# Two eight-expert stages on sorted rows, with the routing inside the attentions ahead of them

## The reference

```python
def _L1_ffn_ref(x, gate_w, w1, w3, w2):          # F = 512
    probs = jax.nn.softmax(jnp.einsum('btd,de->bte', x, gate_w), axis=-1)
    expert_weights, expert_indices = jax.lax.top_k(probs, 2)
    expert_weights = expert_weights / expert_weights.sum(-1, keepdims=True)
    for i in range(8):
        wi = jnp.where(expert_indices == i, expert_weights, 0.0).sum(-1)
        h = jax.nn.silu(x @ w1[i]) * (x @ w3[i])
        out = out + (h @ w2[i]) * wi[..., None]
...
def _L2_ffn_ref(x, Wg, W1, W2, W3):              # H = 256
    top_v, top_i = jax.lax.top_k(jnp.einsum('bsd,ed->bse', x, Wg), 2)
    probs = jax.nn.softmax(top_v, axis=-1)
    for e in range(8):
        w_e = jnp.sum(probs * (top_i == e), axis=-1)
        h1, h2 = x @ W1[e].T, x @ W2[e].T
        out = out + ((h1 * jax.nn.sigmoid(h1) * h2) @ W3[e].T) * w_e[..., None]
```

## Time and profile before

| | us |
|---|---|
| median of 3 runs (lowest, highest) | 1563.43 (1560.48, 1563.63) |
| profiled execution | 1563.46 |
| its span, first to last instruction | 1561.6 |

### The profile page before, as it was taken

The page is one execution under the profiler, slowest core; times in us unless marked ns, Lnnn a source line. Parts: engine busy times, 40 slices in busy tenths (PEclk is TensorE's granted clock), DMA queues, the critical chain, the costliest instruction groups (busy, mean ns, idle before and its releaser), DMA issues. The chain is left out here.

```text
span 1561.6 us, 24205 instructions
## 1 busy us (share of the span) xinstructions
PE 1265.0 (81%) x7182; PEld 1030.1 (66%) x7182; DVE 986.5 (63%) x2041; ACT 723.0 (46%) x1276; POOL 625.1 (40%) x614
## 2 busy tenths in 40 slices
PE   5976499997996899712997596999945759999997
PEld 3873388887564699711886285788723548787875
DVE  6546688885324467560665655677668777777775
ACT  3444367664332555331554253555433325555553
POOL 3205443340000233154333332299824127676665
PEclk9997699997997999855999698799956569999999
DMA  7800011100000000221111620222212024343433
GB/s 202 205 1 0 21 36 41 40 25 0 0 1 0 21 1 0 81 100 52 40 45 32 174 42 21 69 81 87 83 42 84 1 73 129 114 129 116 126 116 102
DMA packets 77282, 98.89 MB, mean 63 GB/s; under 512 B 15226, under 2 KB 41213, under 8 KB 77194
## 3 DMA queue, kind: packets, MB, share of 16 engines
q1 hardware_dynamic: 73490, 92.69, 20.5%
q0 software_dynamic: 2272, 4.24, 0.8%
q10 hardware_dynamic: 1440, 0.98, 0.3%
HBM read 77.87 MB, written 14.16 MB: 59 GB/s over the span
## 5 line engine op out<-in xcount | busy, mean ns | idle before, releaser
L2675 POOL TENSOR_TENSOR e_h<-e_h,e_gate 128x512 f32<-128x512 f32 x128 | 187.9, 1484 | 143.8 <-DVE e_h L2727 87.9
L2732 DVE TENSOR_TENSOR e_h_low<-e_h,e_h_high 128x512 fp32r<-128x512 f32 x132 | 117.2, 888 | 74.4 <-ACT e_h_high L2662 74.2
L2662 ACT ACTIVATE e_h_high<-e_h 128x512 fp32r<-128x512 f32 x132 | 83.5, 633 | 95.8 <-POOL e_h L2675 88.1
L2727 DVE TENSOR_TENSOR e_h<-e_s,e_ps_b 128x512 f32<-128x512 f32 x132 | 89.3, 677 | 13.1 <-ACT e_s L2647 7.2
L1320 PE MATMUL u_ps_o<-u_vaug,u_pT 128*128 128x72 f32 x768 | 97.1, 270 | 0.0
L1320 PEld LDWEIGHTS u_ps_o<-u_vaug,u_pT 128*128 128x128 f32 x768 | 93.5, 192 | 0.0
L2647 ACT ACTIVATE e_s<-e_ps_a 128x512 f32<-128x512 f32 x132 | 77.7, 589 | 31.0 <-PE e_ps_a L1683 27.4
L1251 POOL TENSOR_TENSOR u_kbd<-u_keys,groupmask 96x512 fp32r<-96x512 f32 x60 | 62.9, 1067 | 62.4 <-DMA u_keys<-s_k 36.9
L1347 ACT ACTIVATE u_sm<-u_sm 128x512 f32<-128x512 f32 x96 | 60.6, 631 | 53.5 <-DVE u_sm L1379 52.8
L1377 DVE TENSOR_REDUCE u_mx<-u_ps_s 128x2 f32<-128x512 f32 (+1 forms) x96 | 66.2, 689 | 21.1 <-PE u_ps_s L1302 20.3
L2123 POOL DMA_INDIRECT sorted_y<-e_y,e_zb x39 | 37.8, 970 | 89.8 <-DVE e_y L2328 87.4
(11 more groups left out here) (474 smaller groups left out, 3894.4 us busy)
## 6 DMA issues: line engine op xcount, KB each, us to landing
e_gate<-gates_by_expert SPq DMA_DIRECT2D x256, 128.0 KB, 2.9
e_gate<-gates_by_expert SPq DMA_DIRECT2D x32, 256.0 KB, 3.2
a_q<-q_part SPq DMA_DIRECT2D x24, 256.0 KB, 6.4
w_raw<-in_L1w SPq DMA_DIRECT2D x24, 256.0 KB, 4.9
u_qs<-s_q SPq DMA_DIRECT2D x16, 192.0 KB, 2.6
u_keys<-s_k SPq DMA_DIRECT2D x8, 384.0 KB, 3.5
w_w<-in_L2w SPq DMA_DIRECT2D x24, 128.0 KB, 2.6
sorted<-blank SPq DMA_DIRECT2D x1, 2535.0 KB, 15.7
```

The lines of the kernel that those rows point to most:

```text
L2662: nc.scalar.activation(h_parts[k % 3][0][:, :], h[k % 3][:, :], ACT.Copy).then_inc(high_ready, 1)
L2675: nc.gpsimd.tensor_tensor(h[c % 3][:, :], h[c % 3][:, :], gate[pair % SLOTS][:, :], ALU.mult)\
L2727: nc.vector.tensor_tensor(h[c % 3][:, :], s[c % 3][:, :], ps_b[c % 3][:, :], ALU.mult)\
L2732: nc.vector.tensor_tensor(h_parts[k % 3][1][:, :], h[k % 3][:, :], h_parts[k % 3][0][:, :], ALU.subtract).then_inc(low_ready, 1)
```

## The change

Both eight-expert stages use `experts_sorted`; the second one's dense form is gone. The routing leaves the stage and becomes a class `Router`, which works group by group (four tiles) and is called from every engine's step of the attention ahead: step t takes the statistics of tile t-4, and each group runs through variance, normal rows, transposes, logits, pick, rank and place over the following steps. Three groups' routing and two groups' scatters fall into the attention; the rest (steps 20 to 27) is done at the head of `experts_sorted`. So the passes `n5_` and `n7_` are gone. Each expert now owns a region of 2048 rows (plus 128) in the sorted list, since places are handed out before all counts are known; the list grows from 39 to 135 times 128 rows, there are two lists, and a block's start is read from a second table, one load per block. The list is laid out so that a row's place needs only the counts so far.

The router needs a PSUM bank. In the wide attention the transposes get one bank in place of two, so they go in halves, each waiting until ACT has emptied the bank; in the narrow one the ring has two banks in place of three. All loops over tiles are written out. The weights of the wide attention are loaded at the pass ahead of it rather than in the first narrow attention; four of the first stage's eight experts' weights, and all eight of the second's, are loaded during the attention.

```diff
+SORTED_ROWS = SORT_E * REGION + (SORT_E - 1) * P
...
+    def dve(self, dve, t):
+        nc = self.nc
+        if 4 <= t < TILES + 4:
+            dve.drain()
+            nc.vector.bn_stats(self.stats[:, t - 4, :], self.x[:, t - 4, :])
+        if t % 4 == 3 and 7 <= t < TILES + 4:
+            self.variance(dve, (t - 7) // 4)
+        if t % 4 == 0 and 8 <= t < TILES + 8:
+            self.normal_rows(dve, (t - 8) // 4)
+        if t % 4 == 2 and 10 <= t < TILES + 8:
+            self.pick(dve, (t - 10) // 4)
+        if t % 4 == 3 and 11 <= t < TILES + 8:
+            self.places(dve, (t - 11) // 4)
+        if t == TILES + 7:
+            self.block_table(dve)
...
+    def pe(self, pe, t):
+        nc, E = self.nc, SORT_E
+        n = GROUP * E
+        if t % 4 == 1 and 9 <= t < TILES + 8:
+            g = (t - 9) // 4
+            pe.wait_ge(self.normed, g + 1)
+            if g > 0:
+                pe.wait_ge(self.index_ready, g)
+            for j in range(GROUP):
+                last = nc.tensor.transpose(self.ps[:, j * P:(j + 1) * P], self.rows[0][:, g * GROUP + j, 0:D], self.ident)
+            last.then_inc(self.turned, 1)
+        if t % 4 == 2 and 10 <= t < TILES + 8:
+            g = (t - 10) // 4
+            pe.wait_ge(self.z_out, g + 1)
...
+        if t % 4 == 3 and 11 <= t < TILES + 8:
+            g = (t - 11) // 4
+            pe.wait_ge(self.picks_ready, g + 1)
...
+    def pool(self, pool, t):
+        if t < 12:
+            return
+        g, tile = (t - 12) // 4, t - 12
+        if t == 12:
+            pool.wait_ge(self.prefilled, 32)
+            pool.wait_ge(self.dest_ready, 1)
+        if t % 4 == 0:
+            pool.wait_ge(self.index_ready, g + 1)
+            pool.wait_ge(self.copied, g + 1)
+        for k in range(PICKS):
+            self.nc.gpsimd.indirect_dma_start(
+                out=self.sorted_dram, out_offset=bass.IndirectOffsetOnAxis(ap=self.index[:, tile, k:k + 1], axis=0),
...
+    RING = 3 if router is None else 2
...
-        ps_t = m.ps("ps_t", 1024)
+        ps_t = m.ps("ps_t")
+        if router is not None:
+            router.bank(m.ps("ps_n"))
...
+                for half in range(2):
+                    if live(t, 3):
+                        wait(pe, pT_ready, 2 * (t - 3) + half)
...
+                if router is not None:
+                    router.pe(pe, t)
                 if live(t, 4):
-                    pe.wait_ge(pT_ready, t - 3)
+                    pe.wait_ge(pT_ready, 2 * (t - 3))
...
+            sp.wait_ge(router.table_ready, 1)
             sp.wait_ge(scattered, 16 * PICKS * TILES)
...
-                sp.dma_start(zb[q % NZ][:, :, :], src).then_inc(zb_loaded[q % NZ], 16)
+                for i in range(BATCH):
+                    j = q * BATCH + i
+                    row = sp.value_load(router.table[0:1, 1, j:j + 1], min_val=0, max_val=SORTED_ROWS - P)
+                    sp.dma_start(zb[q % NZ][:, i, :], sorted_dram[bass.ds(row, P), :]).then_inc(zb_loaded[q % NZ], 16)
...
+            pe.wait_ge(router.table_ready, 1)
+            pe.wait_ge(scattered, 16 * PICKS * TILES)
+            keep_busy(nc, ps_h[0], ones_b, 8)
             turn_rows(0)
...
+            router.dve(dve, TILES + 4)
+            weights.make_low(dve, 0)
+            router.dve(dve, TILES + 6)
+            router.dve(dve, TILES + 7)
+            for e in range(1, E):
                 weights.make_low(dve, e)
...
-                                 blank[:, :].unsqueeze(1).broadcast_to([P, BLOCKS, ROW])).then_inc(prefilled, 16)
+                                 blank[:, :].unsqueeze(1).broadcast_to([P, SORTED_ROWS // P, ROW])).then_inc(prefilled, 16)
...
-            weights = SortedWeights(nc, mw, 4, A["L1w1"], A["L1w3"], A["L1w2"])
+            weights = SortedWeights(nc, mw, 4, 4, A["L1w1"], A["L1w3"], A["L1w2"])
...
-            normalise(nc, "n5_", x, idn, root_ln, zT, gate_w=gate1, logits=logits[8], then=ACT.Exp,
-                      loads=weights.first_loads, rows=rows[0])
...
+                normalise(nc, "n4_", x, idn, root_ln, zT, then=ACT.Exp,
+                          loads=load([(t, A["L1" + k]) for k, t in wide1.items()], wide_loaded))
+                kT_all, vT_all = ml.sb("kT", [P, 8, B * KEYS]), ml.sb("vT", [P, 8, B * KEYS])
+                arrive(nc, wide_loaded, 16 * len(wide1))
...
+                attend_wide(nc, "t1_", x, wide1, zT, kT_all, vT_all, idn, neg1, ident_b[:, :], loads=loads, router=router)
+            weights.make_room(mw)
+            experts_sorted(nc, "e1_", x, weights, idn, ones_b[:, :], router, rows, drams[0], signals[0])
...
-            weights = StreamedExperts(nc, mw, zero[:, 0:1], 8, 2, A["L2w1"], A["L2w3"], A["L2w2"])
-            z = [mw.sb(n, [P, TILES * P], F32R) for n in ("z_high", "z_low")]
-            normalise(nc, "n7_", x, idn, root_ln, zT, gate_w=gate2, logits=logits[8], then=ACT.Exp, parts=z,
-                      loads=weights.first_loads, meanwhile=weights.first_splits)
-            experts_gated(nc, "e2_", x, z, logits[8], rank, weights, idn, gates_dram, zT,
-                          lambda sp: many.load_piece(sp, 0))
+            weights = SortedWeights(nc, mw, 2, 8, A["L2w1"], A["L2w3"], A["L2w2"])
...
+                attend_small(nc, "t2_", x, small2, st, idn, ident_r[:, :], groupmask[:, :], HD ** -0.5, ones_b[:, :],
+                             loads=weights.first_loads, router=router)
+            weights.make_room(mw)
+            experts_sorted(nc, "e2_", x, weights, idn, ones_b[:, :], router, rows, drams[1], signals[1],
+                           lambda sp: many.load_piece(sp, 0))
```

More of the change, by code:

```diff
@@ L2029, in experts_sorted @@
         m = Memory(nc, stack, tag)
-        sh = [P, TILES, E]
-        first, second, rest, key, place = (m.sb(n, sh) for n in ("first", "second", "rest", "key", "place"))
-        chosen = m.sb("chosen", sh, BF16)
-        mx1, mx2, top, share1, share2 = (m.sb(n, [P, TILES]) for n in ("mx1", "mx2", "top", "share1", "share2"))
-        slot = [m.sb(f"slot{k}", [P, TILES]) for k in range(PICKS)]
-        index = [m.sb(f"index{k}", [P, TILES], U32) for k in range(PICKS)]
-        count, over, ends, begins = (m.sb(n, [P, E]) for n in ("count", "over", "ends", "begins"))
-        summed_ends = m.sb("summed_ends", [P, E, E])
-        passed = m.sb("passed", [1, BLOCKS, E])
-        expert = m.sb("expert", [1, BLOCKS])
-        table = m.sb("table", [1, BLOCKS], I32)
         zb = [m.sb(f"zb{i}", [P, BATCH, ROW]) for i in range(NZ)]
@@ L2296, in _ @@
-            nc.vector.tensor_reduce(expert[:, :], passed[:, :, :], X, ALU.add)
-            dve.drain()
-            nc.vector.tensor_scalar(table[:, :], expert[:, :], float(E - 1), float(weights.span), ALU.min, ALU.mult)\
-                .then_inc(table_ready, 1)
-            for e in range(E):
+            nc.vector.memset(scratch[:, :], 0.0).then_inc(scratch_ready, 1)
+            router.dve(dve, TILES + 4)
+            weights.make_low(dve, 0)
+            router.dve(dve, TILES + 6)
+            router.dve(dve, TILES + 7)
@@ new lines, in build @@
+            rows = [mw.sb(f"rows{k}", [P, TILES, ROW]) for k in range(PICKS)]
+            router = Router(nc, mw, x, zT, idn, gate2[:, :], sort, rows, sorted_dram[1], prefilled, signals[1][0])
+            router.span = weights.span
+            with ExitStack() as inner:
+                ml = Memory(nc, inner, "a2_")
+                st = Stacked(ml, q_dram, k_dram)
+                open_small(nc, "n6_", x, idn, root_ln, zT, small2, st, ctx2T, groupmask[:, :], takes[:, :])
+                attend_small(nc, "t2_", x, small2, st, idn, ident_r[:, :], groupmask[:, :], HD ** -0.5, ones_b[:, :],
+                             loads=weights.first_loads, router=router)
@@ L2983, in build @@
         finish()
+        late.close()
+        narrow.close()
 def lay_out(i):
```

498 lines of the change are left out of this document (317 added, 181 removed).

## The result

The changed kernel takes 1539.79 us (median of four runs, 1533.72 to 1544.32) against 1563.31 for the kernel before: a ratio of 0.9851 (95% interval 0.9807 to 0.9895), 23.5 us less. Forecast were 54 us less, 1509. The way was right, the size was not: less than half of it came. Of the runs of the experiments, one of the kernel with its transfers in pairs took 2321.57 us at a lower mean clock (0.812) and is left out of what is said of it.

What follows compares the result with a forecast made beforehand. It took PE to bound the wide attention and gated stage, and a wait to fill 667 to 734 us. Terms 16 - 48 + 1.5 + 15 - 38.5 = -54 made 1563.5 into 1509; own range 1490 to 1530.

Steps and rivals of the forecast that it cites:

- Narrow attention, +15: Narrow attention: routing between batches adds 4 to 5 us for each of two pairs, 6 at the end; bounds 5 and 28.
- the rival on the clock: Wide attention: PE's clock falls while it waits for normal rows and picks; 1592 us in all, chance 0.05.
- Wide attention, +16: Wide attention: routing adds 3.6 us of PE work, 2 of waits and 10.4 at the end; bounds 6 and 30.
- the 5.6 of the full steps: Wide attention's full steps: two groups' PE work, 3.6 us, and PE's waits for DVE and the half-emptied bank, 2.
- the 10.4 of the last group: Wide attention's end: waits, logits, pick, ranks, statistics, variance and places, in or right behind the last tile's way, 10.4 us.
- Rival 4: The rival on the clock: 7.55 us more per tile at the lower level, +83 for eleven steps, 1592; chance 0.05.
- Heads, 36: Head of each eight-expert stage, last addition of the attention to first block: 36 us; first stage from 84.2, bounds 28, 47.
- The one stall by a train of splits: Heads: back-to-back weight splits on DVE hold off one of the last scatters, 5.6 us, as a 6.60 us scatter did before.
- The upper bound of 47 for two stalls: Head of the first stage: 47 us if two stalls come, against 36 with one.
- Second stage, -38.5: Narrow attention's last addition to the next pass: 132.6 us for 171.1, from head 36, blocks 76 and tail.
- The block pace, 2.0: Second stage's blocks: 2.0 us each, held by the single bank of the product down; bounds 1.5 and 2.9.
- Weights and fills: Wide attention's weights loaded at the pass ahead: +1.5 us, 0 to 4; list fills end near 160, 27 early: 0.

Runs made afterwards that it cites:

- splits: Changed kernel with one weight split left ahead of each head's last scatters, one once they landed, five between the first blocks: 1538.24 us, ratio 0.9835 to the kernel before.
- late: Changed kernel with the wide attention's router products behind the output and value products, and ScalarE's copy of rows one step later in both stages: 1530.94 us, ratio 0.9799.
- the fillers: Changed kernel plus unread TensorE products ahead of waits in the narrow attention, the wide attention's last four steps and both heads: 1540.96 us, ratio 0.9849.

## Why the prediction was wrong, step by step

*Narrow attention, +15: the step that failed.* It measured +31.2, above its bound of 28. The working added the router's instructions at the full clock, so what the lower clock costs stood at nothing; the rival on the clock was put in the wide attention, where I found 2 us of slack a step. Here the clock fell to 0.50 for the rest of the attention: TensorE was busy 90.6 us, against 80.0 in the short execution of the same attention ("splits") and 71.3 with the transfers in pairs and the ranking later (clock 0.95), with practically the same products (524 or 525). The second thing put at nothing is the train of transfers, "behind its own work" on POOL: the engines wait at it. In sizes, as these executions compare, 10.2 of the 31.2 us are the first fall of the clock (102.2 to 92.0), 4.9 the trains (92.0 to 87.1), and 16.1 are left. That this is near the 15 is partly luck: those 87.1 us still have some 22 at the lower clock (0.84 in 930 to 940 is a fall near 937), which the working did not have in it. With the ranking moved too (and one ScalarE copy) the attention takes 84 to 86 us, +13 to +15, at 0.95 to 0.98. Why the first fall comes in some executions and not in others stays open.

*Wide attention, +16: mis-sized.* It measured +24.4. The addition of the twelfth tile, in the kernel before, the changed one and "late":

```profile
633.53 0.28 DVE L1018 TENSOR_TENSOR x<-x,t_ps_o 128x128 f32 x1
```
```profile
644.26 0.28 DVE L1334 TENSOR_TENSOR x<-x,t_ps_o 128x128 f32<-128x128 f32 x1
```
```profile
641.30 0.28 DVE L1335 TENSOR_TENSOR x<-x,t_ps_o 128x128 f32<-128x128 f32 x1
```

From the first query (522.0, 523.3, 521.4) that is 111.5, 121.0 and 119.9 us: 9.5 us had come by then, for the 5.6 of the full steps, and 14.9 in the last four tiles, for the 10.4 of the last group. Those 10.4 were worked out as if beside the last tiles; the order puts the router's waits ahead of the output products and a copy ahead of ScalarE's copies out of PSUM. With both moved the end takes 7.2 more than before and the steps 8.4, 15.6 in all: that this meets the 16 is luck of two errors that cancel. The clock fell in the last steps (0.72 in 650 to 660), but that was not the cause, as the fillers show. Rival 4's own case, the lower clock for eleven steps, did not come.

*Heads, 36: measured 40.9 and 40.3.* The one stall by a train of splits was right in place and size (6.99 and 6.70 us for the forecast 5.6 more than 0.97), and the experiments show its cause. Missing were 2.8 us until the last places in the first head (13.8 for 11) and 4.6 in the second (15.6), behind the meeting of the engines. Four slowed scatters in the first head (1.44 to 1.75 us, three of them beside splits whose weights came late) are about the 2 us allowed for. The upper bound of 47 for two stalls is a slip: by the same terms it is 42.

*Second stage, -38.5: measured -31.5.* 4.3 us of the 7 are its head. The block pace, 2.0, was right, and the single bank is what holds it at 2.00 and not at 1.77. Of the rest, 1.6 lie in the first and last block (the clock is 0.59 in 1017.8 to 1024.2) and 1.0 in the tail.

*Weights and fills:* +1.3 for +1.5, and the fills in time.

## What to carry to other kernels

Work that is put into another stage's idle time has to be priced at the clock which that stage keeps with it: look for the stage where TensorE already waits a little, and not only for the one with the most work. Put a helper's products behind those of the host step that don't need them, and send its transfers in small lots. A train of VectorE instructions with two SBUF inputs beside GpSimd transfers wants a pause here and there.

## What the runs showed of the hardware that was not expected

- While a train of eight row transfers goes out in the narrow attention, ScalarE and VectorE wait for as long as 6.92 and 4.58 us (1.90 and 2.46 in "splits", where the clock had not fallen before), ended by something the profile calls remote. All nine profiles with such trains have waits that end so in that attention; none of the seven without them has, the sixteen transfers in pairs among them. By what path is open.
- The same attention, with the same wait of 0.89 us, kept the lower clock to its end in one profiled execution, was back at the full clock some 7 us later in another ("late", one copy moved) and did not lose it there in a third ("splits"): 102.2, 92.7 and 92.0 us. The Trainium skill, page "TensorE: Matmul & The Clock Gate", section "A second HAM failure mode: psum-queue depth-cycling", tells of a kernel whose short idle times between groups of products let the clock swing; the rows here agree in that it fell behind a wait of 0.89 us, but they also have the same wait without a fall.
- Emptying VectorE's pipeline between splits, which adds waiting to VectorE, made the program 9 us faster (1536.28 against 1545.21 on the same chip).
